# Cross-attention weights turned in ten chunks of 128 columns instead of by 16 heads of 77

## The chip, the cores and the metric

The kernel runs on one core of a Trainium2 chip (TensorE, VectorE, ScalarE, GpSimd, SyncE and 16 DMA engines). It is one program with one launch. The metric is device time in microseconds.

## What is computed

One decoder layer on x of 2 x 1024 tokens of width 256:

```python
x = x + distance_attention(layernorm(x))        # 16 heads of 64, weights 1/(eps + |q - k|)^2
x = x + cross_attention(layernorm(x), ctx)      # 16 heads of depth 16, ctx has 77 rows per batch
x = x + moe(layernorm(x))                       # 8 experts, best 2 of each token
```

The part that matters here, for each token tile of 128:

```python
logits = einsum('bhqd,bhkd->bhqk', q, k) / 4 + mask * -1e9   # 16 heads x 77 keys
attn = softmax(logits)
out = einsum('bhqk,bhkd->bhqd', attn, v)                     # 16 heads x 16 values
x = x + out @ Wo.T + bo
```

## The kernel before

All data of the layer is fp32. The five engines run programs of their own, in order, tied by semaphores; the order of the work is written out by hand.

The first stage (to about 900 us) is the distance attention, a loop over 32 pairs of (batch, two heads). In `pair(p)` TensorE makes the distances of pair p + 1 while it multiplies the weights of pair p with the values; VectorE guards the distances (L998) and sums half of the weights (`add_second`, L987), GpSimd sums the other half (L1630), ScalarE does the roots, logarithms and exponentials (L1475, L1481, L1483). In the same loop VectorE gates the result of the pair before (`gate`, L1016), and SP stores it to `h_t` (`store_pair`, L296).

In the last pair (`ahead=0`) TensorE first runs `context()`: the keys and values of ctx for the cross-attention, from `ctx_sb` and `w_x_sb` (L428 the keys, L432 the values, into `ps_s`). VectorE's `context()` stands between `add_first` and the sums of the last pair: it waits for all of TensorE's `context()` (`kv_mm`), then adds the key bias (L1025), spreads the keys into a block matrix `k_blk` (L1030) and writes the values with a last column of ones into `v_x` (L1033). SP's queue has, in this order: the store of pair 29, the store of pair 30 (it waits for the gate of pair 30), the load of x into `x_sb` (L343), the router's constants and w_out (behind the last sums), and the first tile of `h_t` (L351).

The second stage goes over 16 token tiles of 128 rows as a pipeline of four sub-stages that `step(t)` weaves on each engine: output projection and layer norm of tile t, queries and logits of tile t - 1, softmax weights times values of tile t - 2, router logits of tile t - 3. Tiles 4 to 15 are a loop, those before and behind it are written out. For the tile t - 2 TensorE turns the exponentials `lg` (128 tokens x 16 heads x 77) head by head with 16 transposes in four calls of `turn_p` (L674), each into half of `ps_p`. ScalarE copies calls 0 and 2 to `p_t` (L1498), VectorE calls 1 and 3 (L1163, `probs_t`). A call waits for the copy that frees its half. `x_values` (L685) multiplies each head's `p_t` (77 keys x 128 tokens) with its 17 columns of `v_x`; column 17 is the sum of the weights, by which `divide` (L1169, L1171) divides. The products are woven between the eight products of `attn_out` (L630). The other lines of this stage that the prediction names: `turn_x` (L641), `copy_xt` (L1135), `query` (L648) and its copy `copy_xq` (L1140), `logits` (L663), mask and row maximum (L1150, L1157), the subtraction on GpSimd (L1684), the exponential (L1527), the square sum on ScalarE (L1522), the roots of both norms (L1503, L1505), `norm_x` (L1131), `expert_in` (L1201), the turn of the result (L693) and `x_out` (L699).

After that come the router and the expert stage, to the end.

Of the kernel before, what the change touches and what calls it, by code (L numbers as in the profile page):

```python
# [5 lines left out]
ALU = mybir.AluOpType  # L6
# [32 lines left out]

LOGITS = ((0, 0, 0, 6), (1, 0, 6, 2), (1, 2, 8, 4), (2, 0, 12, 4))  # L40
# [10 lines left out]
C_ID, C_SQ, C_ONES, C_SK, C_ROWS, C_LO, C_HM, C_IOTA, C_UNIT, C_W = 0, 128, 256, 320, 322, 323, 324, 332, 340, 341  # L51
# [7 lines left out]
def constants(np):  # L59
# [13 lines left out]
    c[:, C_UNIT] = 1.0  # L73
    return c
# [18 lines left out]
def program(nc, x, ctx_t, mask, w_in, b_in, w_out, w_x, b_cols, rows_in, gate_w, w1, w2, w3, consts, r_consts, out):  # L93
    with ExitStack() as ctx:
# [24 lines left out]
        raw_qk = sb("raw_qk", [P, DC, 2, P])  # L119
        raw_vg = sb("raw_vg", [P, DC, 2, P])  # L120
# [30 lines left out]
        ctx_sb = sb("ctx_sb", [P, DC, B * KC])  # L151
# [6 lines left out]
        v_x = sb("v_x", [KC, B, XH, XD + 1])  # L158
# [15 lines left out]
        p_t = vg[0:KC].rearrange("p a t -> p (a t)").rearrange("p (h t) -> p h t", t=P)  # L174
# [19 lines left out]
        def take(n):  # L194
# [66 lines left out]
                 "x1b_ok", "sub_ok", "base_ok", "top_ok", "topi_ok", "topf_ok", "dlt_ok", "pe_ok", "pw_ok", "wf_ok",  # L261
# [7 lines left out]
        C_IN, CST_IN = 16 * (DC + 4 + 1 + 4 + 1 + 1), 16 * (1 + 8)  # L269
# [5 lines left out]
        def _(sp):  # L275
# [34 lines left out]
            for c in range(DC):  # L310
                sp.dma_start(ctx_sb[:, c], ctx_t[c * P:(c + 1) * P]).then_inc(S_.c_in, 16)
# [94 lines left out]
        def _(pe):  # L406
# [15 lines left out]
            def context():  # L422
                pe.wait_ge(S_.c_in, C_IN)
                pe.wait_ge(S_.max_ok, NB * PAIRS)
                for b in range(B):
                    for c in range(DC):
                        for cc in range(DC):
                            pe.matmul(ps_s[:, 0, (b * DC + c) * KC:(b * DC + c + 1) * KC], w_x_sb[:, 1, cc, c * P:(c + 1) * P],  # L428
                                      ctx_sb[:, cc, b * KC:(b + 1) * KC], start=cc == 0, stop=cc == DC - 1)
# [236 lines left out]
            def turn_p(i, k, n):  # L666
                if k == 0:
# [3 lines left out]
                if n >= 1 or k >= 2:  # L671
                    pe.wait_ge((S_.pta_ok, S_.ptd_ok)[k % 2], 2 * i + k // 2)
# [1116 lines left out]
```

## Time and profile before

| | |
|---|---|
| median of 3 runs | 1581.67 us (1579.9 to 1582.06) |
| profiled execution: time, span | 1582.67 us, 1580.8 us |
| mean granted TensorE clock | 0.966 of 2.4 GHz |
| TensorE busy | 1420.2 us (90%) |
| VectorE, ScalarE, GpSimd busy | 1045.0, 927.3, 648.9 us |

Times in the profile are counted from the start of the span. A clock of 1.00 is 2.4 GHz and 0.50 is 1.2 GHz. An fp32 matmul shows as two instructions, a transpose as one.

### The profile page before, as it was taken

The page shows a single profiled execution, that of the slowest core. Times are in us where ns is not written, and L with a number is a line of the kernel's source. Part 1 is how long each engine was busy: PE and PEld are TensorE (multiplying, and loading weights), DVE is VectorE, ACT ScalarE, POOL GpSimd, SP SyncE. Part 2 cuts the span into 40 slices and gives each one's busy share as a digit, 9 for nine tenths or more (in the row PEclk, how much of TensorE's full clock was granted, in tenths as well). Part 3 has the DMA queues.
Part 4 walks back from the last instruction along what each step waited for, and adds up shares of the span by engine and source line. Part 5 has one row for each costly group of instructions (what it writes and reads, how often), then busy time and mean ns, then how long its engine had stood idle before and what let it go on. Part 6 is the DMA issues. An engine that isn't in the chain of part 4 may idle for free. (4 is left out here: it accounts for less than half of the span.)

```text
span 1580.8 us, 23151 instructions
## 1 busy us (share of the span) xinstructions
PE 1420.2 (90%) x7425; PEld 902.6 (57%) x7426; DVE 1045.0 (66%) x1406; ACT 927.3 (59%) x646; POOL 648.9 (41%) x484
## 2 busy tenths in 40 slices
PE   6899999999999999999998569999984799999995
PEld 4555555555555555554554157777764566676664
DVE  7878998889888988898887726666665322222221
ACT  1879888988998899889989602222221122222221
POOL 5255456545554555455543512212220233333331
PEclk9899999999999999999999879999995899999998
DMA  4000000000000000000000313111120134233312
GB/s 145 14 1 15 27 27 13 13 27 27 13 13 27 27 13 13 27 27 13 7 14 14 113 40 109 44 42 53 46 81 14 22 87 139 35 82 81 88 30 70
DMA packets 67483, 66.90 MB, mean 42 GB/s; under 512 B 5152, under 2 KB 59936, under 8 KB 67424
## 3 DMA queue, kind: packets, MB, share of 16 engines
q1 hardware_dynamic: 60160, 56.58, 11.0%
q0 software_dynamic: 7296, 9.97, 3.8%
q8 instruction: 16, 0.26, 0.1%
q14 instruction: 11, 0.09, 0.0%
HBM read 48.70 MB, written 19.92 MB: 43 GB/s over the span
## 5 line engine op out<-in xcount | busy, mean ns | idle before, releaser
L1630 POOL TENSOR_TENSOR v_aug<-v_aug,wts 128x1024 f32<-128x1024 f32 x96 | 254.8, 2654 | 250.1 <-ACT wts L1483 245.5
L998 DVE TENSOR_SCALAR wts<-ps_s,k 128x1024 f32<-128x1024 f32 x240 | 297.2, 1280 | 85.4 <-PE ps_s L538 64.5
L1475 ACT ACTIVATE wts<-wts 128x4096 f32<-128x4096 f32 (+1 forms) x80 | 231.8, 2935 | 88.5 <-DVE wts L998 68.8
L553 PE MATMUL ps_o<-wts,g_r 128*64 128x512 f32 x1024 | 251.4, 614 | 11.3 <-ACT wts L1483 11.2
L1481 ACT ACTIVATE wts<-wts,eps_d 128x4096 f32<-128x4096 f32 (+1 forms) x80 | 241.5, 3019 | 0.2
L1483 ACT ACTIVATE wts<-wts 128x4096 f32<-128x4096 f32 (+1 forms) x80 | 235.1, 2939 | 2.5
L1396 DVE TENSOR_TENSOR wts<-rinv,ps_s 128x352 f32<-128x352 f32 x76 | 39.6, 521 | 253.7 <-ACT rinv L1548 170.6
L793 PE MATMUL ps_s<-wts,qk 128*128 x608 | 197.9, 469 | 3.1 <-issue 2.3
L987 DVE TENSOR_TENSOR v_aug<-v_aug,wts 128x1024 f32<-128x1024 f32 x96 | 156.1, 1626 | 5.4 <-ACT wts L1483 5.1
L538 PE MATMUL ps_s<-q_hi,k_hi 64*128 64x512 f32 x512 | 115.8, 446 | 40.3 <-DVE wts L998 30.1
L793 PEld LDWEIGHTS ps_s<-wts,qk 128*128 128x128 f32 x608 | 110.6, 192 | 64.6 <-issue 16.8
L1548 ACT ACTIVATE rinv<-ps_s 128x352 f32<-128x352 f32 x76 | 35.2, 463 | 176.1 <-PE ps_s L793 176.1
L553 PEld LDWEIGHTS ps_o<-wts,g_r 128*64 128x64 f32 x1024 | 63.6, 138 | 130.6 <-issue 109.8
L1527 ACT ACTIVATE v_aug<-v_aug 128x1232 f32<-128x1232 f32 x16 | 19.7, 1231 | 170.3 <-POOL v_aug L1684 170.3
L538 PEld LDWEIGHTS ps_s<-q_hi,k_hi 64*128 64x128 f32 x512 | 49.2, 185 | 114.0 <-DVE wts L998 81.7
L818 PE MATMUL ps_o<-wts 128*128 x456 | 112.2, 388 | 0.7 <-DVE wts L1404 0.7
L538 PE MATMUL ps_s<-q_lo,k_hi 64*128 64x512 f32 x512 | 102.7, 394 | 0.0
L538 PE MATMUL ps_s<-q_hi,k_lo 64*128 64x512 f32 x512 | 102.5, 392 | 0.0
L538 PE MATMUL ps_s<-q_n,k_n 64*128 64x512 f32 x512 | 102.1, 390 | 0.0
L630 PE MATMUL ps_o<-wts,qk 128*128 128x256 f32 x256 | 83.4, 418 | 14.3 <-DMA qk<-h_t 14.2
L1684 POOL TENSOR_TENSOR v_aug<-v_aug,lmax 128x1232 f32<-128x1232 f32 x16 | 36.0, 2248 | 140.9 <-DVE lmax L1157 140.9
L818 PEld LDWEIGHTS ps_o<-wts 128*128 128x128 f32 x456 | 80.7, 190 | 21.5 <-issue 13.6
(240 smaller groups left out, 2425.2 us busy)
## 6 DMA issues: line engine op xcount, KB each, us to landing
wts<-in_w SPq DMA_DIRECT2D x16, 704.0 KB, 5.4
h_t<-o_raw SPq DMA_DIRECT2D x16, 512.0 KB, 2.6
qk<-h_t SPq DMA_DIRECT2D x16, 512.0 KB, 4.1
wts<-in_w SPq DMA_DIRECT2D x8, 640.0 KB, 7.1
raw_qk<-in_w_in SPq DMA_DIRECT2D x32, 128.0 KB, 2.2
raw_vg<-in_w_in SPq DMA_DIRECT2D x32, 128.0 KB, 2.2
acc<-wts SPq DMA_DIRECT2D x17, 128.0 KB, 1.7
wts<-in_x SPq DMA_DIRECT2D x2, 1024.0 KB, 6.0
```

The source lines that it names most:

```text
L538: mm = pe.matmul(ps_s[:, h, t], k[r], q[r, t], start=i == 0, stop=i == len(terms) - 1)
L553: mm = pe.matmul(ps_o[r, t], v_pair[:, b, r], wts[:, h, b, t], start=b == 0, stop=b == SB - 1)
L630: mm = pe.matmul(bank_a[:, 0:D], h_tile[:, q, :], w_o[:, q, :], start=q == 0, stop=q == H // 2 - 1)
L793: mm = pe.matmul(ps_s[:, k, j * HALF:j * HALF + DEH], y_tt[:, par, c], w12[:, bass.ds(slot, 1), k, c, j * DEH:(j + 1) * DEH], start=c == 0 ...
L818: mm = pe.matmul(ps_o[:, HALF:HALF + D], h_tt[0:m, par, n], w3_sb[0:m, bass.ds(slot, 1), n], start=n == 0, stop=n == NC - 1)
L987: dve.tensor_tensor(acc_w[:, 1], acc_w[:, 1], wts[:, 1, b], ALU.add).then_inc(S_.addb_ok, 1)
L998: dve.tensor_scalar(wts[:, h, b, :], ps_s[:, h, :], k2[:, 2 * b + h:2 * b + h + 1], 0.0, ALU.add, ALU.max).then_inc(S_.max_ok, 1)
L1396: dve.tensor_tensor(h_sb[:, par, t], s_up[:, t], ps_s[:, 1, j * HALF:j * HALF + DEH], ALU.mult).then_inc(S_.hm_ok, 1)
L1475: act.activation(chunk(start, end), chunk(start, end), ACT.Sqrt).then_inc(S_.sqrt_ok, 1)
L1481: act.activation(chunk(start, end), chunk(start, end), ACT.Ln, bias=eps_d[:, 0:1]).then_inc(S_.ln_ok, 1)
L1483: act.activation(chunk(start, end), chunk(start, end), ACT.Exp, scale=-2.0).then_inc(S_.w_ok, 1)
L1630: pool.tensor_tensor(acc_w[:, 0], acc_w[:, 0], wts[:, 0, b], ALU.add).then_inc(S_.add_ok, 1)
```

## The change

The 16 heads x 77 weights of a token row, 1232 columns, are turned in ten chunks of 128 columns (the last has 80) that cross the borders of heads. A chunk touches two or three heads. The values become a block matrix `v_blk`: for each chunk and each head that it touches 17 columns, which are zero in rows that belong to another head; 25 such slots per batch. A chunk's product is 34 or 51 columns wide and adds into one PSUM bank over all ten. `turn_p` is called three times (4, 4 and 2 chunks), ScalarE copies the first and the third, VectorE the second. The set-up in `context()` makes the value rows in chunk order, from a copy of ctx that stands three times side by side (`ctx3`, laid in `norms`), with 40 matmuls, and on VectorE 20 additions, 20 copies of the membership column and 20 products with it. The membership columns come with the constants.

```diff
+XK = XH * KC
+XCH = -(-XK // P)
+XROWS = tuple(min(P, XK - P * j) for j in range(XCH))
+HEAD0 = tuple(P * j // KC for j in range(XCH))
+HEADS = tuple((P * j + XROWS[j] - 1) // KC - HEAD0[j] + 1 for j in range(XCH))
+XSLOT = tuple(sum(HEADS[:j]) for j in range(XCH + 1))
...
# SP
-            for c in range(DC):
-                sp.dma_start(ctx_sb[:, c], ctx_t[c * P:(c + 1) * P]).then_inc(S_.c_in, 16)
...
-            for p in range(PAIRS - 4, PAIRS - 1):
+            for p in range(PAIRS - 4, PAIRS - 2):
                 store_pair(p)
+            sp.wait_ge(S_.split_ok, PAIRS)
+            sp.wait_ge(S_.sqk_ok, PAIRS)
+            for c in range(DC):
+                for r in range(3):
+                    sp.dma_start(ctx3[:, c, :, r * KC:(r + 1) * KC],
+                                 ctx_t[c * P:(c + 1) * P].rearrange("p (b k) -> p b k", b=B)).then_inc(S_.ctx_in, 16)
+            store_pair(PAIRS - 2)
...
# TensorE, context()
-                    for cc in range(DC):
-                        mm = pe.matmul(ps_s[0:KC, 0, HALF + b * D:HALF + (b + 1) * D], ctx_sb[:, cc, b * KC:(b + 1) * KC],
-                                       w_x_sb[:, 2, cc, :], start=cc == 0, stop=cc == DC - 1)
+                    for j in range(XCH):
+                        k0, rows = P * j % KC, XROWS[j]
+                        h0, h1 = HEAD0[j], HEAD0[j] + HEADS[j]
+                        out = ps_s[0:rows, 1, b * HALF + XSLOT[j] * XD:b * HALF + XSLOT[j + 1] * XD]
+                        for cc in range(DC):
+                            mm = pe.matmul(out, ctx3[:, cc, b, k0:k0 + rows], w_x_sb[:, 2, cc, h0 * XD:h1 * XD],
+                                           start=cc == 0, stop=cc == DC - 1)
...
-            def turn_p(i, k, n):
+            def turn_p(i, g, n):
...
-                if n >= 1 or k >= 2:
-                    pe.wait_ge((S_.pta_ok, S_.ptd_ok)[k % 2], 2 * i + k // 2)
-                for j in range(HPB):
-                    mm = pe.transpose(ps_p[0:KC, (k % 2) * HALF + j * P:(k % 2) * HALF + (j + 1) * P], lg[:, HPB * k + j, :], ident)
+                if n >= 1 or g == 2:
+                    pe.wait_ge((S_.pta_ok, S_.ptd_ok, S_.pta_ok)[g], (2 * i, i, 2 * i + 1)[g])
+                for j in range(4 * g, min(4 * g + 4, XCH)):
+                    at = (g % 2) * HALF + (j % 4) * P
+                    mm = pe.transpose(ps_p[0:XROWS[j], at:at + P], lg_flat[:, P * j:P * j + XROWS[j]], ident)
...
# TensorE, x_values(i, e0, e1, n)
+                for j in range(e0, e1):
+                    if j == 0:
+                        pe.wait_ge(S_.pta_ok, 2 * i + 1)
+                    if j == 4:
+                        pe.wait_ge(S_.ptd_ok, i + 1)
+                    if j == 8:
+                        pe.wait_ge(S_.pta_ok, 2 * i + 2)
+                    w = XD + 1
+                    mm = pe.matmul(bank_x[:, HEAD0[j] * w:(HEAD0[j] + HEADS[j]) * w], p_t[0:XROWS[j], j, :],
+                                   v_flat[0:XROWS[j], bass.ds((i >> 3) & 1, 1), XSLOT[j] * w:XSLOT[j + 1] * w],
+                                   start=j == 0, stop=j == XCH - 1, skip_group_check=True)
...
# TensorE, step()
-                woven(0, 0, 2)
+                woven(0, 0, 1)
                 if s3:
                     turn_p(t - 2, 2, n - 2)
-                    turn_p(t - 2, 3, n - 2)
-                woven(1, 2, 4)
+                woven(1, 1, 3)
                 if s2:
                     query(t - 1)
-                woven(2, 4, 6)
+                woven(2, 3, 5)
                 if s2:
                     logits(t - 1, n - 1)
-                woven(3, 6, 8)
-                woven(4, 8, 10)
-                woven(5, 10, 13)
-                woven(6, 13, 16)
+                woven(3, 5, 6)
+                woven(4, 6, 8)
+                woven(5, 8, 9)
+                woven(6, 9, 10)
...
# VectorE
-            dve.memset(v_x[:], 1.0)
...
-                    vv = dve.tensor_tensor(v_x[:, b, :, 0:XD], ps_s[0:KC, 0, HALF + b * D:HALF + (b + 1) * D].rearrange("p (h d) -> p h d", d=XD),
-                                           brow[0:KC, 1].rearrange("p (h d) -> p h d", d=XD), ALU.add)
+                    for j in range(XCH):
+                        rows, h0, h1 = XROWS[j], HEAD0[j], HEAD0[j] + HEADS[j]
+                        src = ps_s[0:rows, 1, b * HALF + XSLOT[j] * XD:b * HALF + XSLOT[j + 1] * XD]
+                        vv = dve.tensor_tensor(v_blk[0:rows, b, XSLOT[j]:XSLOT[j + 1], 0:XD], src.rearrange("p (h d) -> p h d", d=XD),
+                                               brow[0:rows, 1, h0 * XD:h1 * XD].rearrange("p (h d) -> p h d", d=XD), ALU.add)
+                vv.then_inc(S_.k_ok, 1)
+                dve.wait_ge(S_.k_ok, 2)
+                member = cst[:, C_VM:C_VM + XSLOT[-1]].unsqueeze(2)
+                for b in range(B):
+                    for j in range(XCH):
+                        rows, at = XROWS[j], slice(XSLOT[j], XSLOT[j + 1])
+                        dve.tensor_copy(v_blk[0:rows, b, at, XD:XD + 1], member[0:rows, at])
+                        vv = dve.tensor_tensor(v_blk[0:rows, b, at, 0:XD], v_blk[0:rows, b, at, 0:XD],
+                                               member[0:rows, at].broadcast_to([rows, HEADS[j], XD]), ALU.mult)
                 vv.then_inc(S_.kv_ok, 1)
...
# VectorE, step()
                 if s3:
-                    probs_t(t - 2, 1, n - 2)
+                    probs_t(t - 2, n - 2)
                 if s4:
                     norm_x2(t - 3, n - 3)
                 if s2:
                     copy_xt(t - 1)
-                if s3:
-                    probs_t(t - 2, 3, n - 2)
```

## Rows read from the trace of the kernel before

**Rows 1.** The page: busy us, share of the span and instructions of each engine.

```profile
PE 1420.2 (90%) x7425; PEld 902.6 (57%) x7426; DVE 1045.0 (66%) x1406; ACT 927.3 (59%) x646; POOL 648.9 (41%) x484
```

**Rows 2.** Stretches: us from:to, length, busy us and count by engine, clock, DMA share, GB/s.

```profile
1055.50:1072.20 16.70, 15.28 (x94) 12.37 (x94) 11.05 (x31) 4.30 (x11) 3.70 (x4) 1.00 0.15 47
1172.40:1181.00 8.60, 7.38 (x54) 6.32 (x52) 5.63 (x15) 1.60 (x5) 0.73 (x2) 1.00 0.09 30
1181.00:1185.40 4.40, 2.26 (x12) 1.40 (x10) 3.06 (x8) 1.19 (x1) 2.25 (x1) 0.89 0.00 0
1190.00:1196.00 6.00, 6.00 (x31) 6.00 (x30) 1.17 (x2) 0.89 (x4) 0.00 (x0) 0.50 0.13 44
899.00:901.00 2.00, 0.00 (x0) 0.00 (x0) 2.00 (x1) 0.00 (x0) 1.10 (x1) 1.00 1.06 356
```

**Rows 3.** The chain of waits in one iteration of the tile loop: start us, us, what.

```profile
1056.44 0.70 DVE vg L1163
...
1057.18 0.66 PE ps_p L674 x4
...
1066.87 0.27 DVE den L1169
```

**Rows 4.** The timeline of that iteration: start us, us, instructions, idle before and releaser.

```profile
1055.58 0.70 PE L630 MATMUL ps_o<-wts,qk 128*128 128x256 f32 x2 [0.36 <-DMA qk<-h_t]
...
1057.37 0.41 DVE L1135 COPY norms<-ps_o 128x256 f32<-128x256 f32 x1
...
1057.65 0.40 ACT L1522 ACTIVATE qk_sq<-qk_sq 128x256 f32<-128x256 f32 x1
...
1058.48 1.14 PE L648 MATMUL ps_o<-norms,w_x_sb 128*128 128x128 f32 x8
...
1058.84 0.48 DVE L1201 SCALAR_TENSOR_TENSOR qk_sq<-qk_sq,r,brow 128x256 f32<-128x256 f32 x1 [0.27 <-ACT r L1505]
...
1059.66 0.61 DVE L1140 TENSOR_SCALAR norms<-ps_o,b_qk_x 128x128 f32<-128x128 f32 x2 [0.34 <-PE ps_o L648]
...
1065.07 1.44 DVE L1157 TENSOR_REDUCE lmax<-v_aug 128x16 f32<-128x1232 f32 x1
...
1068.10 0.41 SPq L351 DMA_DIRECT2D qk<-h_t  x1
...
1070.45 0.20 ACT L1505 ACTIVATE r<-r 128x1 f32<-128x1 f32 x1
...
1070.95 0.40 DVE L1131 TENSOR_SCALAR norms<-k_sq,mv,r 128x256 f32<-128x256 f32 x1
```

**Rows 5.** The timeline of the set-up in the last pair.

```profile
865.12 1.86 PEld L428 LDWEIGHTS ps_s<-ctx_sb,w_x_sb 128*128 128x128 f32 x16 [0.81 <-issue]
...
872.61 0.91 DVE L1025 TENSOR_SCALAR k_raw<-ps_s,b_qk_x 128x77 f32<-128x77 f32 x4
873.55 2.93 DVE L1030 TENSOR_TENSOR k_blk<-k_raw,cst 128x616 f32<-128x616 f32 x4
...
876.40 0.74 DVE L1033 TENSOR_TENSOR v_x<-ps_s,brow 77x256 f32<-77x256 f32 x2
...
877.43 4.53 DVE L987 TENSOR_TENSOR v_aug<-v_aug,wts 128x1024 f32<-128x1024 f32 x2 [0.28 <-ACT wts L1483]
...
886.77 4.54 DVE L987 TENSOR_TENSOR v_aug<-v_aug,wts 128x1024 f32<-128x1024 f32 x2 [4.81 <-ACT wts L1483]
...
891.22 3.38 DVE L1016 TENSOR_TENSOR o_raw<-o_raw,vg 128x1024 f32<-128x1024 f32 x1
```

**Rows 6.** The timeline of SP's queue behind pair 30's store.

```profile
895.12 0.40 SPq L343 DMA_DIRECT2D wts<-in_x  x1
```

**Rows 7.** The chain of waits at the entry of the tile stage.

```profile
902.19 7.45 DMA qk<-h_t
...
941.59 1.25 PE ps_p L674 x8
```

**Rows 8.** The timeline of the exit of the tile stage.

```profile
1190.01 5.99 PE L685 MATMUL ps_s<-v_x,vg 77*128 77x17 f32 x28
```

More of the change, by code:

```diff
@@ L73, in constants @@
     c[:, C_UNIT] = 1.0
+    for j in range(XCH):
+        for i in range(HEADS[j]):
+            c[:XROWS[j], C_VM + XSLOT[j] + i] = (P * j + np.arange(XROWS[j])) // KC == HEAD0[j] + i
     return c
@@ L118, in program @@
         rstd = sb("rstd", [P, NT])
-        raw_qk = sb("raw_qk", [P, DC, 2, P])
-        raw_vg = sb("raw_vg", [P, DC, 2, P])
+        raw = sb("raw", [P, 2, DC * 2 * P])
+        raw_qk, raw_vg = (raw[:, k].rearrange("p (c h n) -> p c h n", c=DC, h=2) for k in range(2))
         wqk_hi = sb("wqk_hi", [P, DC, 2, P], F32R)
@@ L670, in turn_p, with x_values @@
                         pe.wait_ge(S_.rln_ok, PAIRS)
-                if n >= 1 or k >= 2:
-                    pe.wait_ge((S_.pta_ok, S_.ptd_ok)[k % 2], 2 * i + k // 2)
-                for j in range(HPB):
-                    mm = pe.transpose(ps_p[0:KC, (k % 2) * HALF + j * P:(k % 2) * HALF + (j + 1) * P], lg[:, HPB * k + j, :], ident)
-                mm.then_inc(S_.pt_mm, 1)
-            def x_values(i, h0, h1, n):
-                if h0 == 0:
-                    if n >= 1:
-                        pe.wait_ge(S_.x2_ok, i)
-                for h in range(h0, h1):
-                    if h % HPB == 0:
-                        k = h // HPB
-                        pe.wait_ge((S_.pta_ok, S_.ptd_ok)[k % 2], 2 * i + k // 2 + 1)
-                    mm = pe.matmul(bank_x[:, h * (XD + 1):(h + 1) * (XD + 1)], p_t[:, h, :],
-                                   v_x[:, bass.ds((i >> 3) & 1, 1), h, :], start=True, stop=True)
-                if h1 == XH:
+                if n >= 1 or g == 2:
[3 more added lines that the diff above has]
+                    mm = pe.transpose(ps_p[0:XROWS[j], at:at + P], lg_flat[:, P * j:P * j + XROWS[j]], ident)
+                mm.then_inc(S_.pt_mm, 1)
+            def x_values(i, e0, e1, n):
+                if e0 == 0 and n >= 1:
+                    pe.wait_ge(S_.x2_ok, i)
+                for j in range(e0, e1):
[9 more added lines that the diff above has]
+                                   start=j == 0, stop=j == XCH - 1, skip_group_check=True)
+                if e1 == XCH:
                     mm.then_inc(S_.avx_mm, 1)
@@ L1157, in mask_max, with probs_t @@
                 dve.tensor_reduce(lmax[:], lg, AX.X, ALU.max).then_inc(S_.lmax_ok, 1)
[L1159 to L1160 removed]
+            def probs_t(i, n):
+                dve.wait_ge(S_.pt_mm, 3 * i + 2)
                 if n >= 1:
                     dve.wait_ge(S_.avx_mm, i)
[L1163 to L1164 removed]
+                dve.tensor_copy(p_t[:, 4:8, :].rearrange("p j t -> p (j t)"), ps_p[:, HALF:2 * HALF]).then_inc(S_.ptd_ok, 1)
             def divide(i):
@@ L1492, in _, with probs_t @@
             rows(PAIRS - 1)
-            def probs_t(i, k, n):
-                act.wait_ge(S_.pt_mm, 4 * i + k + 1)
+            def probs_t(i, g, n):
+                act.wait_ge(S_.pt_mm, 3 * i + g + 1)
                 if n >= 1:
                     act.wait_ge(S_.avx_mm, i)
-                act.activation(p_t[:, HPB * k:HPB * (k + 1), :].rearrange("p h t -> p (h t)"), ps_p[0:KC, 0:HALF],
+                j0, j1 = 4 * g, min(4 * g + 4, XCH)
+                act.activation(p_t[:, j0:j1, :].rearrange("p j t -> p (j t)"), ps_p[:, 0:(j1 - j0) * P],
                                ACT.Copy).then_inc(S_.pta_ok, 1)
```

29 lines of the change are left out of this document (16 added, 13 removed).

## The prediction

> **What bounds the kernel now.** I began with the page. TensorE is busy 90% of the span [rows 1], but that is a mean over stages, so the stages were read one by one: which wait ends last in each. The change touches two. One is the stage of sixteen token tiles (about 925 to 1205 us), a software pipeline whose iterations repeat every 16.70 us (the first stretch is cut to one) at the full granted clock of 2.4 GHz [rows 2]. The other is the set-up of the cross-attention operands inside the last pair of heads (865 to 895 us).
>
> The chain of waits of one iteration [rows 3] shows that TensorE does not bind alone: the chain runs through VectorE up to its copy at 1056.44, on to the last four transposes of `turn_p` (1057.18), which wait for that copy to free the upper half of `ps_p`, then through TensorE to the divide at 1066.87, and back to VectorE. The timeline [rows 4] adds what is late next: the row maximum (L1157, 1065.07 + 1.44 = 1066.51) ends 0.36 us before the divide starts. That small number caps the gain.
>
> At the set-up VectorE does all of `context()` before its second sum: to 876.40 + 0.74 = 877.14, then L987 after 0.28 us of idleness; after two sums it waits 4.81 us for the weights of the next blocks; from there on to 901 it has no gap [rows 5]. Its gating product (L1016, 891.22 + 3.38 = 894.60) releases SP's store of pair 30, and behind that store in SP's queue stands the 2 MB load of x [rows 6], and then w_out and the first tile of h_t. From 895 to 909 the DMA engines are full (a share of 1.06 [rows 2]), and the tile, issued last at 902.19, lands at 909.65 [rows 7], when TensorE starts the stage. So whatever delays that gating product delays the stage.
>
> **The change, part by part.** *Values.* 16 heads are 32 TensorE instructions (fp32 shows as two per matmul); ten chunks are 20. At the exit 28 take 5.99 us at the lower clock level [rows 8], 0.214 each, so 0.107 at the upper; I take 0.11. The load of 128 columns sets this step, not the stream: L428 streams 77 columns behind the same load and steps by 1.86/16 = 0.116 [rows 5], and 17 columns become 34 or 51. So 12 x 0.11 = 1.3 us of TensorE less per tile, 0.2 of it ahead of the logits, 1.1 behind them. The bound against it: 51 columns cost 20 x 0.11 x (51 - 17)/128, or 0.6 us more.
>
> *Transposes.* 16 of 77 columns become ten of up to 128; an instruction each, so six less. Four take 0.66 us in the chain with their start-up; at the 0.11 us step that is 0.65 us less. The weights grow from 77 to 128 columns: L685 and L648, with 128 columns [rows 4, 8], show 0.11 to 0.14 each, so ten of them are dearer by at most 0.1 us in all. The Trainium skill (TensorE: Matmul & The Clock Gate, LDWEIGHTS) says that a weight load costs by its columns and not by its contraction rows, which speaks against the wider transposes: ten loads of 128 columns are 1280, sixteen of 77 are 1232. If loads set the pace, the transposes would save nothing, the entry below would gain 0.9 us and not 2.5, and the time would come out 1.6 later, plus what the exit loses. The sum goes by the rows instead.
>
> *Evictions.* Two by ScalarE and two by VectorE of 512 columns (0.69 us each on VectorE) become two by ScalarE (512 and 256) and one by VectorE. Their time goes by columns (128x256 takes 0.41 in L1135, 77x512 0.70: 1.1 ns a column), so I count 128 partitions like 77.
>
> *Steady step.* The wait for the upper half is gone and turn_p's last part is two transposes that wait for a copy long finished. What is late next is `copy_xt`, 1057.37 + 0.41 = 1057.78, for which the query product waits: it starts near 1057.83 instead of 1058.48 and ends 0.65 earlier, near 1058.97. Its eviction (L1140) then waits for `expert_in` instead, in order on VectorE and behind ScalarE's L1522. L1522 started at 1057.65 behind a ScalarE copy that now ends earlier; it can start at 1057.48. So `expert_in` (1058.84) runs 1058.67 to 1059.15, and L1140 goes at 1059.16 instead of 1059.66: 0.50 us. Logits, mask and row maximum follow at their present distances. The divide then starts right behind the maximum, 0.33 sooner, since the value products, the last thing it waited for, end 1.1 us sooner still. But the layer norm's L1131 (1070.95) waits also for L1505 of ScalarE, 1070.45 + 0.20, which hangs on the exponential and so on the maximum: measured from the maximum's end that is 4.14, plus 0.04 of hand-over, against 0.03 + 4.08 by the divide. It takes back 0.07. Period 16.70 - 0.50 - 0.33 + 0.07 = 15.94, 0.76 less; twelve iterations: 9.1 us. Bounds: 0.5 (L1522 does not move, so L1140 gains 0.33, and the hand-over to L1131 takes 0.13 as from L1505 to L1201) to 1.0 (0.65 and 0.36 both whole), 6 to 12 us.
>
> *Entry and exit.* At tiles 2 and 3, unrolled, TensorE itself is the chain. In the first, six of the eight transposes go at 1.25/8 = 0.156 us [rows 7], 0.94, and one head, 2 x 0.156 = 0.31: 1.3 us. In the second, at full clock, six at 0.105 and a head at 0.22, plus 0.3 that the divide handed on: 1.2. Together 2.5 us, bounds 2 to 4. At the last loop step 0.3 (the 0.33 above) without a next eviction. At the exit the clock is granted at 0.50 [rows 2] and the last 28 value instructions end at 1196.0, with the divide behind them: 0.214 each. Six transposes and twelve value instructions fewer at that step, 18 x 0.214: the divide comes 3.8 us sooner; bounds 2 to 4 (a wait for the copies that come between). Sum of gains: 9.1 + 2.5 + 0.3 + 3.8 = 15.7 us.
>
> *Set-up.* TensorE: four value products (8 instructions of 256 columns) become 40 (80 instructions of 32 or 48). 16 loads take 1.86 us now [rows 5], 0.116 each; 80 take 9.3. They start where the keys' loads end, near 866.9, so the product is done near 876.2, and VectorE, which waits for all of it, starts L1025 at 876.3 and not 872.61. TensorE's products for the weight blocks wait behind it too, but like VectorE they run in bursts with gaps, the next at 886.77: two bursts of some 4 us from 876.2 end at 884; covered. VectorE: L1025 0.91, L1030 2.93 (beside GpSimd from 877.5, where L987 takes 2.27 for 1024 columns, twice what 1.1 ns a column gives, so up to 2 more: I take 1.5), then 20 additions out of PSUM. The same form now (L1033) takes 0.74 for two of 256 columns, (0.74 - 2 x 0.27)/2 = 0.10 fixed each; L1025 shows (0.91 - 4 x 0.08)/4 = 0.15. With 0.042 for 40 columns that is 2.8 or 3.8; I take 2.8, the same form. Then 20 copies and 20 products in SBUF of 2 to 48 columns, which no row has: L1030 shows 2.93/4 - 0.64 = 0.09 fixed, so 20 x 0.09 + 20 x 0.13 = 4.4 (bounds 3 with 0.06, and 7 with 0.15). End: 876.3 + 0.91 + 2.93 + 1.5 + 2.8 + 0.1 (a wait for its own sums) + 4.4 = 888.9. The Trainium skill (VectorE: DVE Perf Modes, the errata section) gives 120 cycles fixed from PSUM and 58 in SBUF at 0.96 GHz; by it the 60 operations are an estimated 3.3 + 3.3 us, 0.6 less than mine.
>
> Then four sums (2.27 each beside GpSimd) and the gating product (3.38), 12.5 us, less 0.7 because GpSimd's own sums end near 900: to 900.7 instead of 894.6. The load of x and all behind it start 6.1 us later, and with full DMA engines the first tile lands 6.1 us later. The last two sums, then nearly alone, end by 904, ahead of the tile's issue at 908.3. Cost 6.1 us; bounds: VectorE done at 885.5 and the first sum alone, 2.5; done at 892, 8.5. The six ctx transfers stand on SP behind pair 29's store, which a gate a whole pair earlier releases, and their waits are for work of pair 31's projections, older still: free. The store of pair 30 behind them waits for VectorE until 894.6 anyway. The dropped memset and the wider constants lie at the start beside the load of x: 0.
>
> Sum: -15.7 + 6.1 = -9.6 us. The profiled run is 1582.67 us, its span 1580.8, the median 1581.67; the difference goes on the median: 1572.1 us.
>
> **Rivals.** (1) *Set-up hidden* (chance 0.15): the small operations take 0.06 us each and GpSimd does not slow them; the delay is 2.5 or less, time 1581.67 - 15.7 + 2 = 1568 or lower. For it: the 4.81 us gap. Against it: VectorE's late start by TensorE alone costs 3.7. (2) *Set-up eats it* (0.17): 0.2 us for each of 60 small operations and contention with GpSimd; VectorE done at 893 or later, delay 9 or more, and with the low bound of the loop's gain (6) the time is 1581.7 - 12.6 + 9 = 1578; against it, L1033's 0.37 us for 256 columns. (3) *The tile's load binds the loop* (0.05): TensorE waits 0.36 us for it at 1055.58 already. From there, the new order needs 1.65 to the query, 2.1 + 2.3 to the logits' end, 3.7 to the last output product, then 0.6 to the issue and 4.1 to landing (from 1068.10): 14.5, under 15.9. If landing took 2.2 us longer, the step's gain would be gone: 1581.67 - 2.5 - 3.8 + 6.1 = 1581, or 1577 with half of it. (4) *The clock* (0.07), the other side: with 13.3 us of work in 15.9 TensorE idles more. Where it was busy 2.26 of 4.40 us the grant fell, 0.89 in the mean, and was then 0.50, the 1.2 GHz level [rows 2]. If the grant sank for half of the loop's time, a step would be 13.3/0.75 = 17.7 us, 12 x 1.8 = 21 us more than my sum, 1593. It decides from about a third of the time low (13.3/0.83 = 16.0 is still free; 13.3/0.8 = 16.6 adds 8). Against it: 1172.4 to 1181, busy 7.38 of 8.60 us, kept 1.00, and the new step is as busy. The Trainium skill (TensorE: Matmul & The Clock Gate, Part 1) says that activity releases the throttle and idleness brings it back; it names this risk, and the rows give its price.
>
> **Numbers.** My forecast holds 0.56: 1569 to 1576. Range for 8 in 10: 1564.5 (rival 1 with more of the loop gain) to 1578. What a measurement of this kernel can tell from no change is about 0.2%, 3 us. Faster by more: the forecast, rival 1, most of rival 2 and half of rival 3, 0.85. Within: 0.07. Slower: rival 4 and a rest of rival 2, 0.08.
>
> **What would show it.** Period 15.9 us in the tile stage; no wait of turn_p on VectorE; L1140's successor directly behind expert_in; the divide directly behind the row maximum; 20 value instructions per tile; VectorE's context ending near 888.9, the load of x issued near 901.3 and the first product of the stage near 916; the value run at the exit some 4 us long at 0.50. Wrong would make it: a clock under 1.00 in the loop, small operations above 0.2 us, or value instructions that step by more than 0.12 us.

## The result, and the profile after

The changed kernel takes 1586.18 us in the median (1581.49 to 1587.95, 20 runs), the kernel before 1581.96 (1574.95 to 1586.14, 20 runs): ratio 1.0026, 95% interval 1.0016 to 1.0035. It is slower by 4.2 us, where I had forecast 1572.1. A second comparison (again_after against again_before) gave 1.0040 [1.0026, 1.0054]. The profiled span is 1585.7 us, 4.9 more than before. TensorE has less work, VectorE more [rows 1]:

```profile
PE 1396.7 (88%) x7209; PEld 882.7 (56%) x7210; DVE 1058.1 (67%) x1447; ACT 923.8 (58%) x646; POOL 645.9 (41%) x484
```

Three marks in both traces divide the 4.9 us: the start of the keys' product in the last pair, the first product of the tile stage, and the router's product for the token lists (L775 before, L804 after).

| stretch | before | after | difference | forecast |
|---|---|---|---|---|
| start and pair loop, to the keys' product | 865.12 | 880.39 | +15.3 | 0 |
| set-up, to the first tile's product | 44.7 | 56.0 | +11.4 | +6.1 |
| tile stage, to the token lists' product | 313.2 | 292.2 | -21.0 | -15.7 |
| from there to the end | 357.8 | 357.1 | -0.7 | 0 |

**The pair loop**, which the change does not touch. Two iterations, called a period here, take 53.03 us before, thirteen times over, and 54.12 after, twelve times; the last period after takes 53.12. In one such period VectorE's instructions in the two traces agree within 0.01 us up to its guard behind its sum for block 2. These are VectorE and then GpSimd in the timeline of before, from there on:

```profile
513.75 2.48 DVE L998 TENSOR_SCALAR wts<-ps_s,k 128x1024 f32<-128x1024 f32 x2 [0.20 <-DVE v_aug L987]
...
526.61 1.21 DVE L987 TENSOR_TENSOR v_aug<-v_aug,wts 128x1024 f32<-128x1024 f32 x1
528.91 2.48 DVE L998 TENSOR_SCALAR wts<-ps_s,k 128x1024 f32<-128x1024 f32 x2 [1.09 <-PE ps_s L538]
...
524.22 5.86 POOL L1630 TENSOR_TENSOR v_aug<-v_aug,wts 128x1024 f32<-128x1024 f32 x2 [2.14 <-ACT wts L1483]
```

And the same instructions after:

```profile
523.62 2.48 DVE L1026 TENSOR_SCALAR wts<-ps_s,k 128x1024 f32<-128x1024 f32 x2 [0.31 <-DVE v_aug L1015]
...
536.48 3.44 DVE L1015 TENSOR_TENSOR v_aug<-v_aug,wts 128x1024 f32<-128x1024 f32 x1
540.11 1.28 DVE L1026 TENSOR_SCALAR wts<-ps_s,k 128x1024 f32<-128x1024 f32 x1 [0.20 <-DVE v_aug L1015]
...
533.97 4.86 POOL L1670 TENSOR_TENSOR v_aug<-v_aug,wts 128x1024 f32<-128x1024 f32 x2 [2.02 <-ACT wts L1522]
```

The gap in front of the guard (the number in brackets) is 0.31 us instead of 0.20. The sum for block 5 then takes 3.44 us instead of 1.21, and GpSimd's pair of sums (blocks 6 and 7), which took 5.86, takes 4.86. The two hold each other off: before, VectorE is first and GpSimd waits 1 us, which nothing needs; after, GpSimd is first and VectorE waits 2.2 us, of which 1.1 take the place of its next wait (1.09, for TensorE) and 1.1 lengthen the period. The Trainium skill (SBUF — State Buffer, Who interferes with whom) calls the port pair that the two share an exclusive lock and says that the order of issue decides who blocks; these rows agree.

The last period after shows the same from the other side. The gap is 0.31 us as in the others, but VectorE's sum starts a little sooner: 35.61 us behind the log table's load (ScalarE's change of function table, the zero of a period from here on), where the eleven periods before it have 35.63 to 35.66. It wins, takes 1.21 us, GpSimd's pair takes 6.02, and the period is short again:

```profile
794.19 2.48 DVE L1026 TENSOR_SCALAR wts<-ps_s,k 128x1024 f32<-128x1024 f32 x2 [0.31 <-DVE v_aug L1015]
...
807.05 1.21 DVE L1015 TENSOR_TENSOR v_aug<-v_aug,wts 128x1024 f32<-128x1024 f32 x1
809.35 2.48 DVE L1026 TENSOR_SCALAR wts<-ps_s,k 128x1024 f32<-128x1024 f32 x2 [1.09 <-PE ps_s L563]
...
804.49 6.02 POOL L1670 TENSOR_TENSOR v_aug<-v_aug,wts 128x1024 f32<-128x1024 f32 x2 [1.89 <-ACT wts L1522]
```

**The set-up.** TensorE's products of keys and values, VectorE's `context()` (of the 20 small copies the first and the three long ones), its sums and the gate; then SP's load of x:

```profile
880.39 1.86 PEld L449 LDWEIGHTS ps_s<-norms,w_x_sb 128*128 128x128 f32 x16 [0.81 <-issue]
...
882.24 13.20 PE L457 MATMUL ps_s<-w_x_sb,norms 128*128 128x32 f32 x80
...
895.48 0.91 DVE L1053 TENSOR_SCALAR k_raw<-ps_s,b_qk_x 128x77 f32<-128x77 f32 x4 [7.67 <-PE ps_s L457]
896.42 5.98 DVE L1058 TENSOR_TENSOR k_blk<-k_raw,cst 128x616 f32<-128x616 f32 x4
902.33 2.20 DVE L1066 TENSOR_TENSOR raw<-ps_s,brow 128x32 f32<-128x32 f32 x20
904.56 0.17 DVE L1074 COPY raw<-cst 128x2 f32<-128x2 f32 x1
...
904.93 2.34 DVE L1074 COPY raw<-cst 128x2 f32<-128x2 f32 x1
...
909.46 2.36 DVE L1074 COPY raw<-cst 128x2 f32<-128x2 f32 x1
...
912.02 2.33 DVE L1074 COPY raw<-cst 128x3 f32<-128x3 f32 x1
...
914.73 5.20 DVE L1015 TENSOR_TENSOR v_aug<-v_aug,wts 128x1024 f32<-128x1024 f32 x4
919.84 1.22 DVE L1044 TENSOR_TENSOR o_raw<-o_raw,vg 128x1024 f32<-128x1024 f32 x1
...
921.58 0.40 SPq L362 DMA_DIRECT2D wts<-in_x  x1
```

Counted from the start of the keys' product, the load of x [rows 6] is issued at 41.2 us instead of 30.0, 11.2 later, and the first tile's product comes 11.4 later. The 80 small value products took 13.2 us. The clock fell in their middle, with TensorE busy without a gap. These are two stretches of the same length, with 20 and 13 product instructions (columns as in [rows 2]):

```profile
884.00:886.00 2.00, 2.00 (x20) 2.00 (x19) 0.70 (x1) 2.00 (x2) 0.00 (x0) 0.98 0.00 0
886.00:888.00 2.00, 2.00 (x13) 2.00 (x12) 1.81 (x3) 2.00 (x1) 0.00 (x0) 0.50 0.00 0
```

**The tile loop.** Its period is 15.52 us instead of 16.70, at the same clock [rows 2]:

```profile
1066.00:1081.52 15.52, 12.90 (x79) 10.33 (x78) 10.25 (x29) 3.99 (x11) 3.70 (x3) 1.00 0.16 51
```

One iteration, beside [rows 4]:

```profile
1066.05 1.44 DVE L1199 TENSOR_REDUCE lmax<-v_aug 128x16 f32<-128x1232 f32 x1
...
1071.53 0.41 DVE L1173 TENSOR_SCALAR norms<-k_sq,mv,r 128x256 f32<-128x256 f32 x1
...
1073.62 0.69 DVE L1205 COPY vg<-ps_p 128x512 f32<-128x512 f32 x1 [0.30 <-PE ps_p L700]
1074.55 0.42 DVE L1177 COPY norms<-ps_o 128x256 f32<-128x256 f32 x1
1075.02 1.16 PE L673 MATMUL ps_o<-norms,w_x_sb 128*128 128x128 f32 x8 [0.74 <-DVE norms L1177]
1075.87 0.48 DVE L1242 SCALAR_TENSOR_TENSOR qk_sq<-qk_sq,r,brow 128x256 f32<-128x256 f32 x1 [0.90 <-ACT r L1545]
1076.27 0.60 DVE L1182 TENSOR_SCALAR norms<-ps_o,b_qk_x 128x128 f32<-128x128 f32 x2
...
1081.57 1.44 DVE L1199 TENSOR_REDUCE lmax<-v_aug 128x16 f32<-128x1232 f32 x1
...
1082.92 0.25 DVE L1210 RECIPROCAL den<-ps_s 128x16 f32<-128x16 f32 x1
```

The query (L673) waits for `copy_xt`, its eviction (L1182) stands directly behind `expert_in`, the divide directly behind the row maximum: the order that I forecast. At the exit the last run of value products (L714) has 18 instructions and takes 2.28 us, where 28 took 5.99 [rows 8]. That is not only the smaller number: the clock, 0.50 throughout that run before, is 1.00 here from 1199.94 on. One step earlier it is the other way round, the clock is 0.50 while the logits run (L688), which take 4.03 us instead of 2.34:

```profile
1185.98 4.03 PE L688 MATMUL ps_s<-k_blk,norms 128*128 128x462 f32 x8 [0.32 <-DVE norms L1182]
...
1199.56 2.28 PE L714 MATMUL ps_s<-raw,vg 128*128 128x51 f32 x18
...
1186.29:1189.70 3.41, 3.41 (x8) 2.09 (x7) 0.00 (x0) 0.00 (x0) 0.00 (x0) 0.50 0.22 75
1199.94:1203.36 3.42, 2.94 (x25) 2.57 (x24) 1.84 (x6) 1.15 (x5) 0.72 (x1) 1.00 0.20 67
```

### The profile page after: what moved, and what is told of

Read it like the earlier page. It is cut to its first block and busy times, and to the rows that moved or that the text cites. A ratio compares the mean times of both kernels' runs of the same rounds, so it can differ in the third digit from the quotient of the medians.

```text
span 1585.7 us, 22668 instructions
## 1 busy us (share of the span) xinstructions
PE 1396.7 (88%) x7209; PEld 882.7 (56%) x7210; DVE 1058.1 (67%) x1447; ACT 923.8 (58%) x646; POOL 645.9 (41%) x484
## 5 line engine op out<-in xcount | busy, mean ns | idle before, releaser
L1670 POOL TENSOR_TENSOR v_aug<-v_aug,wts 128x1024 f32<-128x1024 f32 x96 | 240.4, 2504 | 251.7 <-ACT wts L1522 247.1
L1015 DVE TENSOR_TENSOR v_aug<-v_aug,wts 128x1024 f32<-128x1024 f32 x96 | 174.5, 1818 | 0.4
L1662 POOL TENSOR_TENSOR k_sq<-norms 128x1024 f32<-128x1024 f32 x16 | 42.1, 2632 | 124.8 <-DVE norms L957 124.8
```

Of the source, the lines that this page charges most:

```text
L1015: dve.tensor_tensor(acc_w[:, 1], acc_w[:, 1], wts[:, 1, b], ALU.add).then_inc(S_.addb_ok, 1)
L1662: pool.tensor_tensor(k_sq[:], k32[:], k32[:], ALU.mult).then_inc(S_.sqk_ok, 1)
L1670: pool.tensor_tensor(acc_w[:, 0], acc_w[:, 0], wts[:, 0, b], ALU.add).then_inc(S_.add_ok, 1)
```

## The experiments

Eighteen runs follow, two of them of the two kernels again. "Gap" is the idle time in front of the guard behind the sum for block 2, "stretch" the time from the start of the keys' product to that of the first tile's. A ratio is that to the kernel before, measured beside the run, with its 95% interval.

### The same two again, and the moved parts

**again_before**, **again_after**: both kernels unchanged.

> The kernel before, once more. In the first traces two iterations of the pair loop take 53.0 us together in the kernel before and 54.1 us in the changed one, 15.3 us in all before the set-up, though the loop's code is the same. If the pattern is a property of the program (where its start puts the engines, or where its tiles lie), this run shows 53.0 again throughout. If it is drawn anew at each execution, it can show 54.1 or a mixture.

> The changed kernel once more. Property of the program: 54.1 us per two iterations again, set-up product starting near 880. Drawn at each execution: 53.0 or a mixture, the set-up starting between 865 and 880. The set-up itself (first tile of h_t landing some 56 us after the start of the keys' product, against 44.5 before) should repeat in either case.

1582.55 and 1586.54 us; periods 53.03 and 54.12, gaps 0.20 and 0.31, as the first time: the loop's loss belongs to the kernel, not to a run.

**early_only**: the kernel before with what the change moves away from the start, and nothing else of it.

```diff
-            dve.memset(v_x[:], 1.0)
...
-            for c in range(DC):
-                sp.dma_start(ctx_sb[:, c], ...)      # now behind the store of pair 29
...
# constants 25 columns wider, ones written in context()
```

> The kernel before with only what the change does to the start: no memset of v_x there (its ones are written in the set-up), the two ctx loads moved from the start to behind pair 29's store, the constants 25 columns wider. Set-up and tile stage as before. If the start of the program decides the pattern of the pair loop, it takes 54.1 us per two iterations and the time rises by 10 to 15 us. If the merged raw tile and the new places of the tiles decide, it stays at 53.0 and within 2 us of the kernel before.

1594.89 us, ratio 1.0096 [1.0069, 1.0123]; gap 0.31, period 54.13.

**early_restored**: the changed kernel with the memset and the two early loads put back, each into a spare tile; the constants stay wide.

> The changed kernel with the start of the kernel before put back (a memset of a spare tile of v_x's size on VectorE, the two early ctx loads into a spare tile, waited for as before); the late ctx loads and everything else stay. If the start decides: 53.0 us per two iterations and some 15 us less than the changed kernel, near 1571, which is what my sum without the pair loop would give. If the places of the tiles decide: 54.1 and no change.

1572.19 us, 0.9946 [0.9928, 0.9964]; period 53.03. So one of the two moved parts costs some 14 us, the memset or the loads.

### The memset

**memset_gone**: the kernel before, SP and constants as they were, without the memset at the start. **one_tiny_op**: the changed kernel with one column set in its place.

```diff
-            dve.memset(v_x[:], 1.0)
+                dve.memset(v_x[:, :, :, XD:XD + 1], 1.0)      # in context()
```
```diff
+            dve.memset(spare[:], 0.0)      # 128 x 1, before the pair loop
```

> The kernel before without the memset of v_x at the start; the ones are written in the set-up. SP's queue and the constants are those of before. If VectorE's instructions ahead of the loop decide: 0.31 us, 54.1 us per two iterations and 10 to 14 us slower than before (1592 to 1595), like the run that had all three early edits. If the ctx loads or the constants decide: 53.0 and the time of before.

> The changed kernel with one more VectorE instruction ahead of the pair loop: a memset of one column of a spare tile. It takes 0.06 us before x has landed, and nothing else changes. The four traces so far differ in one gap: VectorE's guard of block 4 (TENSOR_SCALAR wts) starts 0.20 us after the sum before it where the program has the memset of v_x, and 0.31 us where it has not. If it is VectorE's number of instructions ahead of the loop that matters (where the loop's code lies), this run shows 0.20, 53.0 us per two iterations and a time near 1572. If the duration of the memset or the early ctx loads matter, it stays at 0.31, 54.1 and 1586.

1597.96 us (1.0112 [1.0087, 1.0137]), gap 0.31, period 54.13; and 1571.47 us (0.9939 [0.9919, 0.9958]), gap 0.20, period 53.03. So it is the memset alone, and it counts by its presence, not by its 0.5 us: a memset of 0.06 us does the same. SP's queue and the constants are cleared.

**before_one_more**, **before_three_more**, **before_seven_more**, **fifteen_more**, **two_gone**: the kernel before with 1, 3, 7 or 15 further memsets of one column ahead of the loop, or without the ones and one of the small constants.

> The kernel before with one further memset of one column behind the start memset: VectorE's loop starts one instruction later in its stream. Two iterations take 53.03 us where the count ahead of the loop is that of the kernel before (five kernels) and 54.12 where it is one less (after, again_after, early_only, memset_gone). If it is only that the count may not be less, it stays at 53.03 and 1581 us. If each place in the stream has a gap of its own, 53.03 us is one value of several: another place can give the 0.31 us in front of another guard, and then anything from 1575 (no second sum of 3.4 us left) to 1597 (a further one, 13 times 1.1 us), each with the gap visible in front of the guard.

> The same with three memsets of one column. If it is only that the count may not be less: 53.03 us for two iterations, 1581 us. If each place has a gap of its own: 51.9 to 54.2 us for two iterations and 1567 to 1597 us, and where it is neither 53.03 nor 54.12 the sums in front of which the 0.3 us stand are others than the guard of the fourth block.

> The same with seven memsets of one column. If the place in the stream counts with a period (lines of eight instructions or a divisor of it), seven more is the same place as one less: the guard of the fourth block follows after 0.31 us, 54.12 us for two iterations, 1595 to 1597 us. If it is only that the count may not be less: 53.03 and 1581 us.

> The kernel before with fifteen memsets of one column behind the start memset. If the place counts with a period of sixteen instructions, this is the same place as one less: 0.31 us, 54.1 us for two iterations, 1593 to 1597 us. If not, 52.6 to 53.03 us for two iterations and 1579 to 1582 us, as with one, three and seven more.

> The kernel before with two instructions fewer ahead of the pair loop: the ones of the values and one of the three small constants are written in the set-up of the tile loop. If fewer instructions than before are what costs, 54.1 us for two iterations and 1595 to 1598 us, as in memset_gone. If it is the place of just one less, the gap of 0.31 us is gone or stands elsewhere: 53.03 us and 1581 to 1584 us.

1579.64, 1579.74, 1581.53 and 1581.56 us with more, all within 0.2% of before, periods 52.6 to 53.05; 1596.82 us with two fewer, gap 0.31, period 54.12. There is no pattern that comes back after 2, 4, 8 or 16 instructions: one or two fewer lose, up to 15 more do not.

### Who goes first

**gpsimd_later**, **gpsimd_much_later**: the changed kernel with one GpSimd memset of 128x1, or 128x256, ahead of its sum for block 7. **sum_later**, **sum_much_later**: the kernel before with one on VectorE, of the same two sizes, ahead of its sum for block 5.

```diff
+                    if b == 7:
+                        pool.memset(spare[:], 0.0)
                     add_block(p, b)
```

> The changed kernel with one memset of one column on GpSimd between its sums for blocks 6 and 7 in each pair, nothing on VectorE. If the loss is the meeting of two sums (in after VectorE's sum for block 5 starts 0.04 to 0.1 us behind GpSimd's sum for block 7 and then takes 3.44 us instead of 1.22), a later GpSimd lets VectorE go first: that sum takes 1.2 to 1.7 us, two iterations 53.0 us, and the kernel 1570 to 1573 us, although the gap of 0.31 us in front of the guard stays. If the loss comes from the place of VectorE's instructions by another way, it stays at 54.1 and 1586 us.

> The changed kernel with a memset of 128 x 256 on GpSimd between its sums for blocks 6 and 7, in place of one column: GpSimd's sum for block 7 should start at 35.8 us or later behind the log table's load, VectorE's for block 5 stays at 35.64 and is first now. If the meeting is the cause, VectorE's sum takes 1.2 to 1.7 us, two iterations 53.0 to 53.2 us, and the kernel 1570 to 1574 us, with 0.31 us still in front of the guard. If not, 54.1 us and 1585 us as in gpsimd_later.

> The kernel before with one memset of one column on VectorE just ahead of its sum for block 5, once in each pair, the start as it was. If 0.1 us are enough to lose the meeting, that sum takes 3.4 us instead of 1.2, two iterations 54.1 us, and the kernel 1593 to 1597 us, with 0.20 us still in front of the guard. If lateness is not the cause, 0.1 us for each iteration at most: 1581 to 1584 us.

> The kernel before with a memset of 128 x 256 on VectorE (0.27 us at the start of the kernel) just ahead of its sum for block 5, in place of one column: VectorE's sum comes at about 35.8 us, behind the start of GpSimd's at 35.56. If the meeting is the cause, it takes 3.2 us or more, two iterations 54.1 to 54.4 us, and the kernel 1593 to 1600 us, with 0.20 us in front of the guard. If not, 0.3 us for each iteration at most and 1581 to 1589 us.

gpsimd_later: 1585.13 us, period 54.12. The memset was too short: GpSimd's sum for block 7 still started first, 35.59 us behind the log table's load against 35.64 for VectorE's, which took 3.44. gpsimd_much_later: 1574.91 us (0.9953 [0.9938, 0.9969]), period 53.14. Its rows, VectorE and then GpSimd:

```profile
517.75 2.48 DVE L1027 TENSOR_SCALAR wts<-ps_s,k 128x1024 f32<-128x1024 f32 x2 [0.31 <-DVE v_aug L1016]
...
530.61 1.22 DVE L1016 TENSOR_TENSOR v_aug<-v_aug,wts 128x1024 f32<-128x1024 f32 x1
...
528.10 2.38 POOL L1671 TENSOR_TENSOR v_aug<-v_aug,wts 128x1024 f32<-128x1024 f32 x1 [2.01 <-ACT wts L1523]
530.41 0.32 POOL L1685 MEMSET spare<- 128x256 f32 x1
530.68 3.40 POOL L1671 TENSOR_TENSOR v_aug<-v_aug,wts 128x1024 f32<-128x1024 f32 x1
```

VectorE's sum starts 0.07 us ahead of GpSimd's and takes 1.22 us; GpSimd's takes 3.40. The 0.31 us stay, and the period is longer than before's by just that 0.11. The two runs with a later VectorE did not give what I expected: 1580.81 and 1582.86 us, ratios 0.9996 [0.9979, 1.0014] and 1.0002 [0.9989, 1.0016], no loss. In sum_later the sum came only 0.01 to 0.03 us later and was still first; in sum_much_later the memset itself was first:

```profile
526.60 0.27 DVE L989 MEMSET spare<- 128x256 f32 x1
526.78 1.16 DVE L990 TENSOR_TENSOR v_aug<-v_aug,wts 128x1024 f32<-128x1024 f32 x1
...
524.10 6.10 POOL L1633 TENSOR_TENSOR v_aug<-v_aug,wts 128x1024 f32<-128x1024 f32 x2 [2.12 <-ACT wts L1486]
```

GpSimd's pair took 6.10 us instead of 5.86, as if it had waited for memset and sum together: VectorE's turn seems to have begun with the memset. If so, the edit did not make VectorE late. Neither run speaks for the meeting or against it.

### The set-up

Both on top of one_tiny_op. **keys_first** signals the keys' product apart, so that VectorE does L1053 and L1058 while TensorE makes the values. **wide_ops** does the 40 copies and products in four.

```diff
+                mm.then_inc(S_.kv_mm, 1)      # behind the keys; VectorE waits for 1, then for 2 ahead of the values
```
```diff
-                    for j in range(XCH):
-                        rows, at = XROWS[j], slice(XSLOT[j], XSLOT[j + 1])
-                        dve.tensor_copy(v_blk[0:rows, b, at, XD:XD + 1], member[0:rows, at])
...
+                    dve.tensor_copy(v_blk[:, b, :, XD:XD + 1], member)
+                    vv = dve.tensor_tensor(v_blk[:, b, :, 0:XD], v_blk[:, b, :, 0:XD],
+                                           member.broadcast_to([P, XSLOT[-1], XD]), ALU.mult)
```

> The changed kernel with the tiny instruction, and the set-up's products signalled in two parts, so that VectorE spreads the keys (L1053, L1058 in the changed kernel's trace: 0.9 and 6.0 us) while TensorE still makes the values. If the set-up's cost is VectorE's time behind the product that ends last: these 6.9 us go from behind the product into its shadow, where GpSimd is idle, and the gate of pair 30 ends 4 to 7 us sooner against the start of the keys' product, the time falls by as much against the tiny run (1565 to 1568). If instead the wait for GpSimd or the DMA queue bind whatever VectorE does: under 2 us.

> The changed kernel with the tiny instruction, and the 20 copies and 20 products in SBUF of the set-up made as 2 and 2 over all 25 slots. In the changed kernel they take 10.2 us, of which three copies of 2.3 us each lie beside running GpSimd sums. If those waits come with each copy that meets a running GpSimd instruction, two copies meet at most two: 1 to 1.5 us of work and at most 4.6 of waits, so the gate ends 4 to 8 us sooner, less what the sums behind it lose by meeting GpSimd (up to 4): 2 to 6 us net. If the stretch costs by the number of elements or GpSimd takes its share anyway: under 1 us.

1569.52 us (0.9932 [0.9906, 0.9958]) and 1567.89 us (0.9919 [0.9895, 0.9943]); stretches 52.9 and 53.7 us against 56.1 in one_tiny_op. (wide_ops' profiled run is 7 us shorter than one_tiny_op's; 4.4 of that lie ahead of the keys' product and are not its own.) Both gained less than the work they save: counted from the keys' product `context()` ended at 27.4 and 27.9 us instead of 34.6 in one_tiny_op, but the next four sums took 9.1 and 9.3 us instead of 5.2, as the wait for GpSimd moved into them. wide_ops, VectorE's timeline:

```profile
885.02 0.19 DVE L1074 COPY raw<-cst 128x25 f32<-128x25 f32 x1
885.11 0.57 DVE L1075 TENSOR_TENSOR raw<-raw,cst 128x400 f32<-128x400 f32 x1
885.59 2.37 DVE L1074 COPY raw<-cst 128x25 f32<-128x25 f32 x1
887.86 0.56 DVE L1075 TENSOR_TENSOR raw<-raw,cst 128x400 f32<-128x400 f32 x1
888.35 9.34 DVE L1017 TENSOR_TENSOR v_aug<-v_aug,wts 128x1024 f32<-128x1024 f32 x4
```

**both_orders**: the two together.

> The changed kernel with the one-column memset ahead of the pair loop, with the keys' product signalled apart, and with the copies and multiplications of the block matrix over all 25 slots at once: the last two took 2.0 and 3.7 us off the median of one_tiny_op (1571.5), and in the traces they shorten the stretch from the keys' product to the first tile's product from 56.1 us to 52.9 and 53.7. If VectorE's own work sets the end of the set-up, the two add up: 1571.5 - 2.0 - 3.7 = 1565.8 us, the stretch about 50.5 us, ratio about 0.990. If GpSimd's sums of the last pair set it (VectorE's last four sums took 5.2 us in one_tiny_op and 9.1 and 9.3 in the other two), the second edit finds nothing left: 1567 to 1569 us and a stretch of 52.5 to 53.5.

1563.22 us (1559.79 to 1567.62), ratio 0.9896 [0.9872, 0.9921], the fastest of all. Neither of my two accounts gave that: the stretch is 48.5 us, 7.7 less than one_tiny_op's and more than the 3.2 and 2.4 of the single edits. `context()` ends 20.7 us behind the keys' product, the gate at 33.2 (before 29.5, one_tiny_op 40.8, keys_first 37.5, wide_ops 38.3). In all five the first tile's product follows the gate's end by 15.2 to 15.4 us, so the gate sets the stretch. The traces show why the two edits gain more together than the sum of each. In `context()` they save 7.2 and 6.7 us, and together 13.9, exactly the sum. The wait for GpSimd that comes back behind it does not add up: of the four sums and the gate two take 3.2 to 3.4 us instead of 1.2 in each single edit (4 us lost), and three with both (6.3 us lost).

## Why the prediction was wrong

**The failed step**: "The dropped memset and the wider constants lie at the start beside the load of x: 0." The constants and the load cost nothing, the memset's absence 15 us (one_tiny_op against again_after: 1571.47 and 1586.54). I had priced the instruction by its own time, which was indeed covered, and not asked what stands on an edge in the 850 us behind it. The chain, as far as shown: all seven runs with fewer instructions of VectorE ahead of the loop than before had 0.31 us in front of the guard, and all but gpsimd_much_later lost; the others had 0.20 where the meeting was the same. With 0.31 VectorE's sum for block 5 starts 35.61 to 35.70 us behind the log table's load (35.9 in the first period) instead of 35.47 to 35.58, while GpSimd's for block 7 stays near 35.6. All 227 meetings of these two sums in the traces, sum_much_later's apart, follow one rule: VectorE wins as long as its start is recorded at most 0.03 us behind GpSimd's, and waits from 0.04 us on. The middle link is shown twice: in gpsimd_much_later, with the gap there and only GpSimd later, the loss was gone but for 0.11 us a period, and so it was in the last period of the changed kernel. In the profiled pair twelve periods by 1.1 us are 13.2 of the 15.3; the other 2.1 stood already ahead of the first period, and the repeated pair does not have them: there thirteen periods were long, and the keys' product came 13.3 us later.

Why the gap is longer can be read from the steps of VectorE's sequencer in the traces. One step of each period takes some 0.12 us more than elsewhere, and it stands at a fixed place of the instruction stream: with two instructions fewer ahead of the loop it is the guard's own (0.18 us instead of 0.07), with one fewer the semaphore wait just in front of it (0.21 instead of 0.09), with one, three and seven more it lies two, four and eight instructions in front of that wait (0.23 instead of 0.12, 0.21 instead of 0.09, 0.20 instead of 0.08), each time while a guard is still running, which hides it. In the kernel before its place is the instruction between, behind the wait for the sum, and no delay is seen there. So each instruction ahead of the loop moves the slow place by one, and of the places seen it costs only at the two between the end of the sum and the guard. What makes the place slow is open. The Trainium skill (Runtime: NRT & Kernel Launch, Instruction fetch mechanics) has engines fetch their instructions in blocks of 256, and the border of a block would be such a place; no run here shows that it is this.

**Set-up: right in kind, too small**, +6.1 forecast, +11.4 measured. By its terms, counted from the keys' product: the 80 loads ran at 0.11 us at first, as forecast, and from 886 at the lower clock level, 3.9 us more than "9.3". My fourth rival had the clock fall in the tile loop, where TensorE idles, and not here, where the profile has it busy throughout. The Trainium skill (TensorE: Matmul & The Clock Gate, Part 1) ties the fall to idleness; the rows show it in busy, narrow products, and the measurement decides. `k_blk` took 5.98 us, 1.6 above my 2.93 + 1.5: of its four operations two took 0.79 us, one 1.68 and one 2.96. The additions took 2.20 (I: 2.8). The 40 copies and products took 10.2 us and not 4.4: 37 of them some 0.09 us apart, 3.2 in all, near the low bound of 3 that I had given, and three copies of two or three columns 2.3 us each, until the GpSimd sum that was running had ended. I had counted contention for the large operation, and none for small ones, which pay the same wait. Against that the four sums and the gate took 6.3 us and not 11.8: the wait was paid earlier. 3.9 + 1.6 - 0.6 + 5.8 - 5.5, less the 0.1 for a wait that did not come, are 5.1, the gate's 11.2 less the 6.1; 0.2 more came between gate and tile. I had misread the price of the meeting, too: the 2.27 us that I took for each sum beside GpSimd are the mean of 1.23 and 3.20 in the trace of before, one sum free and one that waits, and not a slower pace of both. That the gate, SP's store, the load of x and the tile follow one another was right: 11.2 us at the gate and at the load, 11.4 at the tile.

**Steady step: right in order, 0.42 us short.** Period 15.94 forecast, 15.52 measured. From the row maximum's end (1067.49) the norm follows at 4.04 (forecast 4.18), `probs_t` 2.09 behind it (2.18), the query's eviction 2.65 behind that (2.72), the maximum's end 6.74 later (6.85): four pieces of about 0.1 us that I had taken over from [rows 4]. Twelve steps gave 12.8 us, not 9.1. Two of them were 0.6 longer, where the clock was 0.50 for 3.4 us each; before it did not fall in the loop, so that much of my fourth rival came. Value products step by 0.11 us, with 51 columns as with 17, so the bound of 0.6 us against it did not come. Eight transposes take 1.09 us in the loop, with 77 columns of weights (before) as with 128 (after):

```profile
1070.23 1.09 PE L674 MATMUL ps_p<-cst,v_aug 128*77 128x128 f32 x8 [0.51 <-ACT v_aug L1527]
...
1071.21 1.09 PE L700 MATMUL ps_p<-cst,v_aug 128*128 128x128 f32 x8 [0.97 <-ACT v_aug L1567]
```

So the Trainium skill's count of columns (TensorE: Matmul & The Clock Gate, LDWEIGHTS), 1280 against 1232, did not decide; an instruction less was 0.11 us less, as the sum had it.

**Entry and exit.** To the first divide 2.5 us less, as forecast, and 1.6 more in the step behind it, together the upper bound of 4. The exit's last two steps gave 3.8 us, as forecast, but by luck: the first was 1.6 us longer, with the logits at the lower clock, and the second 5.4 shorter, most of its last value products at the upper one, where I had counted 18 instructions at the lower clock throughout.

**Rivals.** None of the four was it, though 2 came in half: the delay of 9 or more did, the low bound of the loop did not. That one_tiny_op, with the pair loop as before, stands 0.6 us from my 1572.1 is no confirmation: 5.3 us more in the set-up and 5.3 less in the tile stage cancel.

## What to carry to other kernels

In a loop where VectorE and GpSimd sum side by side, look in the timeline for pairs of operations that start within 0.1 us of each other and see what the order costs: there a change elsewhere can decide by 0.1 us what then costs 1 us in every round. Compare the two traces first in the stages that were *not* changed. Replace an early instruction that is dropped by another small one and measure both, before the change itself is judged. Many small VectorE operations beside GpSimd should be few wide ones: each can draw the whole wait. But the wait can come back in the next operation (4 of the 6.7 us that wide_ops saved did), so count it for the whole stretch.

## What the runs showed of the hardware

- One VectorE instruction fewer ahead of an 850 us loop: 0.31 instead of 0.20 us in front of one guard, and 15 us in all; 1, 3, 7 or 15 more: nothing. A step of VectorE's sequencer that is 0.12 us longer moves by one instruction with each instruction ahead of the loop (-2, -1, +1, +3, +7).
- By who starts first, a sum of 128x1024 takes 1.22 or 3.44 us on VectorE and 2.4 or 3.40 on GpSimd; a VectorE copy of two columns 0.15 or 2.34.
- The clock fell to the 1.2 GHz level during 80 products of 32 and 48 columns with TensorE busy 2.00 of 2.00 us, in after, one_tiny_op and both_orders alike.
